# A decoder layer on one core: six small sums of weight magnitudes are put later into TensorE's queue

## The chip, the cores and the metric

The kernel is one program on one core of a Trainium2 chip. Its engines are TensorE (PE, with its weight loads shown apart as PEld), VectorE (DVE), ScalarE (ACT), GpSimd (POOL) and SyncE (SP), which issues most of the DMAs. The metric is the device time of one execution in microseconds (us); less is better.

## What is computed

One decoder layer for 2 sequences of 512 rows, width 512, in three parts, each followed by a residual sum and a layer norm:

```
q, k, v = (x @ (codes * scales) + bias for q, k, v)          # 16 heads of 128, weights in fp4 blocks
attn = softmax(q k^T / sqrt(128));  x = ln(x + (attn v) @ (wo_codes * wo_scales) + bo)
s = coef * (x Wq) ctx^T; keep the 54 largest of 1024; x = ln(x + softmax(s) ctx Wo)
x = ln(x + (silu(x Wg) * (x Wu)) @ Wd)                       # 2048 inner columns
```

The change is in the first part alone, the self-attention.

## The kernel before

**Numbers as sums of two.** To keep float32 accuracy with fast matmuls, each operand is split into a high part in a reduced format and a low part, what is left. A product is then three matmuls: high by high, high by low, low by high. Weights that are a code times a power of two fit into the high part whole, and their low part is zero. The kernel finds this out as it runs: `check_lo` notes each low part of a weight, `run_checks` (L235) has ScalarE sum its absolute values over a row (tile `JA` is thrown away, the sum goes to a column of `mag`), and `run_sums` adds the columns over the 128 partitions with a small float32 matmul (L247, `p<-mag,ones`, two passes, so two records) and lets ScalarE reduce the 2 or 4 results to one number, `flag` (L250, output `fsum`). A projection (`mm_if`, and `bias_o` at L468 for the bias row) loads the flag into a register of TensorE's sequencer (L109, TENSOR_LOAD) and branches over the low matmuls when it is zero (L113, COMPARE_AND_BRANCH). With this data it is zero each time.

**Keys.** A key names a piece of weights: `("qk", j)` for the query and key weights of a head, `("v", g)` for the value weights of four heads, `("o", p)` for the output projection weights of two heads, p = 0 to 7. There are 30 keys, and so 30 sums, 8 of them of kind `o`.

**Order.** The program builds one queue per engine, in the order of one Python loop, and each engine runs its queue strictly in that order; semaphores are waited for at the instruction that needs them. The loop runs over i = 0 to 127. A step j = i // 4 handles one head of one sequence, and qt = i % 4 is its quarter (128 query rows). In quarter i TensorE gets, as far as they exist: `proj_qk` for head step j+1 (qt 0 and 1; tile `R`), `av` for step j-1 (qt 0; `PT,V`), `proj_o` for an earlier pair of steps (qt 2 and 3; `WO,OT`), `proj_v` (`WV,R`), the transposes of quarter i (L528, `ident,PR`), and the scores of quarter i+2 (`QK`). Then come, in this order, the splitting of results by VectorE, `run_sums` when qt is 1, 2 or 3, `bias_o` in three quarters (i = 25, 57, 89, each for two p), the softmax exponentials (L511), and `run_checks`.

**ScalarE and VectorE around it.** For each quarter ScalarE writes the high part of the transposed probabilities (L535, `PT<-p`) and VectorE their low part (L538, `PT<-p,PT`); `av` needs all four quarters of both. VectorE writes the low parts of queries and keys (L373). ScalarE also converts the high parts of coming weights (L277).

**Banks.** `fbank()` hands out four accumulator banks in turn (P[4] to P[7]) to the projections, `av`, the sums and `bias_o`; a user waits for what emptied the bank of the user four before it.

**Where the `o` sums stand.** The checks of `("o", p)` are done in quarter i = 16p+6 for p = 0 to 5, a quarter with qt = 2, and the sum follows in the next quarter, i = 16p+7. The first `proj_o` with these weights is in quarter i = 16p+10, and `bias_o` in i = 16p+9 for odd p.

Of the kernel before, what the change touches and what calls it, by code (L numbers as in the profile page):

```python
# [51 lines left out]
def flat(ws):  # L52
    out = []
    for w in ws:
        if w is None:
            continue
        if isinstance(w, list):
            out += flat(w)
        else:
            out.append(w)  # L60
    return out

def decoder_layer(nc, xT, xn, wq, sq, wk, sk, wv, sv, wo, so, bqk, bv, bo,
                  xwq, xwo, ctxT, ctxn, scal, wg, wu, wd, rq, rk, out):
    with ExitStack() as top:
# [6 lines left out]
        def op(q, fn, *waits):  # L73
            return q.add(fn, flat(waits), True)
# [52 lines left out]
        def sbt(ctx, name, shape, dt=F32):  # L127
            return ctx.enter_context(nc.sbuf_tensor(name, shape, dt))
# [20 lines left out]
        fsum = sbt(top, "fsum", [1, 4])  # L149
        flag = sbt(top, "flag", [1, 32])  # L150
# [70 lines left out]
        now = [-1]  # L221
        checks, sums = [], []
# [16 lines left out]
                    sums.append((now[0], key))  # L239

        def run_sums():
            while sums and sums[0][0] < now[0]:
                _, key = sums.pop(0)
                n, col, ts = FL[key]
                k, ps = fbank()
                o = ps[0:1, 0:n]
                t = pe.add(lambda e, o=o, col=col, n=n: e.matmul(o, ones[:, 0:1], mag[:, col % 4, 0:n],  # L247
                                                                 start=True, stop=True),
                           flat([ts, t_one, bank[5 + k]]), True)
                t = op(act, lambda e, o=o, col=col, n=n: e.activation(fsum[:, 0:n], o, ACT.Copy,  # L250
                                                                       accum_out=flag[:, col:col + 1]),
                       t, T.get(("flag", col - 1)))
                bank[5 + k] = T[("flag", col)] = t

        def flag_of(key):
            c = FL[key][1]
# [65 lines left out]
        T = {}  # L322
        bank = [None] * 8
        nf = [1]

        def fbank():
            k = nf[0] % 4 - 1
            nf[0] += 1
            return k, P[5 + k][:, :]
# [769 lines left out]
        for i in range(4 * NJ):  # L1099
# [25 lines left out]
            if qt:  # L1125
                run_sums()
# [29 lines left out]
            if i == 1:  # L1156
                t = op(act, lambda e: e.activation(bv_r[:, :, 0], bv_f, ACT.Copy), T_BIAS)
# [17 lines left out]
            if j == 30 and qt in (1, 2):  # L1175
                for r in (2 * qt - 2, 2 * qt - 1):
                    k, _ = fbank()
# [4 lines left out]
            if i in (123, 124):  # L1182
                for m in (2 * (i - 123), 2 * (i - 123) + 1):
                    k, _ = fbank()
# [3 lines left out]
            if i in (125, 126):  # L1188
                for hf in range(2):
                    k, _ = fbank()  # L1190
# [256 lines left out]
```

How the kernel before makes its waits and increments, by code:

```python
    def emit(self, eng):  # L38
        reached = {}
        for waits, fn, inc in self.items:
            for sem, v in waits:
                if reached.get(id(sem), 0) < v:
                    reached[id(sem)] = v
                    eng.wait_ge(sem, v)
            if fn is None:
                continue
            ins = fn(eng)
            if inc:
                ins.then_inc(self.sem, 1)
# [33 lines left out]
            def load(self, dst, src, *waits, q=sp):  # L83
                self.n += 1
                s = self.sem
                q.add(lambda e: e.dma_start(dst, src).then_inc(s, 16), flat(waits), False)
                return (s, 16 * self.n)
```

## Time and profile before

| | |
|---|---|
| median of 3 runs | 970.06 us (968.97 to 971.03) |
| profiled execution: its own time | 969.82 us |
| profiled execution: span of its instructions | 968.0 us |
| TensorE busy in the span | 928.3 us (96%) |
| DVE, ACT, POOL busy | 577.2, 580.5, 474.3 us |
| granted TensorE clock, mean | 0.993 of full |
| self-attention with the 30 sums | about 37 to 494 us of the span |

The profile is one execution. Rows of the timeline give the start of an instruction or of a run of like instructions, its length, the engine, the line, and in brackets how long the engine had been idle before it and what it then waited for. Matmuls overlap by design, so distances are read from start to start.

### The profile page before, as it was taken

What the parts mean: (1) busy time and instruction counts of PE and PEld (TensorE: products, weight loads), DVE (VectorE), ACT (ScalarE), POOL (GpSimd) and SP (SyncE); (2) the same over time, 40 slices, a digit from 0 to 9 for tenths busy, and PEclk for the clock granted to TensorE, in tenths of its full rate; (3) what the DMA queues carried; (4) which work ended last, traced back from release to release, by engine and by line L of the source; (5) the groups of instructions that cost most, each with busy time, mean ns of one, the idle gap of its engine ahead of it and who ended that gap; (6) DMA issues with size and microseconds to landing.
All of it is one profiled execution on the core that took longest, in us unless ns stands there. A gap on an engine that the chain in (4) does not pass through costs nothing.

```text
span 968.0 us, 13297 instructions
## 1 busy us (share of the span) xinstructions
PE 928.3 (96%) x4516; PEld 752.3 (78%) x4516; DVE 577.2 (60%) x1057; ACT 580.5 (60%) x1201; POOL 474.3 (49%) x375
## 2 busy tenths in 40 slices
PE   9999899999999999999999989899999899999997
PEld 7787678877788776877667777888878788788886
DVE  5666856576566666565676799984878214511114
ACT  4667866687767778687775446544564634443333
POOL 4246642535515456466564347552684652354440
PEclk9999999999999999999999999989999999999999
DMA  6531220122201322122222122231433241243331
GB/s 197 153 108 46 82 88 1 46 71 71 82 17 28 88 58 68 61 65 60 62 66 87 44 66 88 88 98 55 131 110 96 78 142 43 76 133 97 99 87 43
DMA packets 46101, 76.97 MB, mean 80 GB/s; under 512 B 5584, under 2 KB 11216, under 8 KB 45776
## 3 DMA queue, kind: packets, MB, share of 16 engines
q1 hardware_dynamic: 45600, 75.68, 26.4%
q8 instruction: 41, 0.67, 0.3%
q10 hardware_dynamic: 432, 0.39, 0.1%
q14 instruction: 28, 0.23, 0.1%
HBM read 73.69 MB, written 2.36 MB: 79 GB/s over the span
## 4 chain that ended last, share of the span: by engine, by line
PE 81%; DVE 9%; ACT 5%; issue 3%; DMA 1%; POOL 0%; SPq 0%; DVEq 0%; ACTq 0%; POOLq 0%
PE p L99 75%; PE p L528 5%; DVE JK L503 2%; DVE acc L447 1%; ACT PR L511 1%; ACT JA L235 1%; DVE PT L538 1%; DMA acc<-in_xT 1%; DVE m L726 1%; DVE QK L373 1%; DVE st L588 0%; PE p L779 0%; PE p L636 0%; DVE SX L737 0%; DVE SCL L731 0%
## 5 line engine op out<-in xcount | busy, mean ns | idle before, releaser
L503 DVE TENSOR_SCALAR_CACHE_REDUCE JK<-p,ssc 128x512 bf16<-128x512 f32 x112 | 83.8, 748 | 149.4 <-PE p L99 149.0
L654 POOL TENSOR_TENSOR V<-RAW,V 128x512 fp32r<-128x512 f32 x64 | 82.4, 1309 | 143.2 <-ACT V L653 143.2
L444 POOL TENSOR_TENSOR acc<-SX,acc 128x512 f32<-128x512 f32 x52 | 68.7, 1321 | 169.7 <-ACT SX L438 131.2
L99 PE MATMUL p<-R 128*128 128x512 f32 x544 | 136.9, 394 | 2.4 <-DVE V L399 0.8
L99 PE MATMUL p<-QK 128*128 128x512 f32 x384 | 117.4, 414 | 4.5 <-DVE QK L373 4.1
L99 PEld LDWEIGHTS p<-R 128*128 128x128 f32 x544 | 100.9, 188 | 26.8 <-issue 1.4
L511 ACT ACTIVATE PR<-p,nms,ssc 128x512 f32<-128x512 f32 x112 | 87.2, 778 | 57.6 <-DVE JK L503 57.1
L99 PE MATMUL p<-R,V 128*128 128x512 f32 x480 | 112.7, 390 | 0.8 <-ACT C L653 0.8
L99 PEld LDWEIGHTS p<-R,V 128*128 128x128 f32 x480 | 89.9, 188 | 19.8 <-issue 1.2
L275 POOL TENSOR_TENSOR RAW<-RAW,SCL 128x512 f32<-128x512 f32 x65 | 87.8, 1357 | 28.1 <-DMA SCL<-in_so 14.5
L654 POOL TENSOR_TENSOR C<-RAW,C 128x512 fp32r<-128x512 f32 x58 | 76.0, 1323 | 40.3 <-ACT C L653 40.2
L99 PE MATMUL p<-PT,V 128*128 128x512 f32 x384 | 93.5, 392 | 1.9 <-DVE PT L538 1.9
L99 PE MATMUL p<-C 128*128 128x512 f32 x384 | 92.5, 390 | 0.2 <-issue 0.2
L99 PE MATMUL p<-WV,R 128*128 128x512 f32 x368 | 91.1, 394 | 1.4 <-DVE JK L503 1.1
L99 PE MATMUL p<-V 128*128 128x512 f32 (+1 forms) x432 | 91.3, 368 | 0.7 <-POOL V L654 0.7
L887 DVE TENSOR_TENSOR SX<-p,SX 128x512 f32<-128x512 f32 x32 | 22.1, 691 | 116.5 <-PE p L99 115.7
L538 DVE TENSOR_TENSOR PT<-p,PT 128x512 fp32r<-128x512 f32 x128 | 87.4, 683 | 4.9 <-ACT PT L535 4.7
L99 PEld LDWEIGHTS p<-PT,V 128*128 128x128 f32 x384 | 70.7, 188 | 20.2 <-issue 2.5
L99 PEld LDWEIGHTS p<-V 128*128 128x128 f32 x432 | 74.9, 190 | 14.2 <-ACT V L653 1.1
L99 PEld LDWEIGHTS p<-C 128*128 128x128 f32 x384 | 71.7, 188 | 15.3 <-issue 0.6
L99 PEld LDWEIGHTS p<-WV,R 128*128 128x128 f32 x368 | 67.7, 188 | 19.0 <-issue 3.0
L528 PE MATMUL p<-ident,PR 128*128 128x128 f32 x512 | 77.6, 274 | 0.0
(170 smaller groups left out, 1665.6 us busy)
## 6 DMA issues: line engine op xcount, KB each, us to landing
RAW<-in_wg SPq DMA_DIRECT2D x32, 256.0 KB, 2.8
RAW<-in_wu SPq DMA_DIRECT2D x32, 256.0 KB, 2.6
RAW<-in_ctxn SPq DMA_DIRECT2D x32, 256.0 KB, 2.8
RAW<-in_wd SPq DMA_DIRECT2D x32, 256.0 KB, 2.7
RAW<-in_wq SPq DMA_DIRECT2D x19, 256.0 KB, 2.7
RAW<-in_wk SPq DMA_DIRECT2D x18, 256.0 KB, 2.6
RAW<-in_wv SPq DMA_DIRECT2D x16, 256.0 KB, 2.7
RAW<-in_wo SPq DMA_DIRECT2D x16, 256.0 KB, 4.7
```

What stands on the lines that cost most here:

```text
L99: return e.matmul(outp, a, b, start=st, stop=sp_)
L235: T[("JA",)] = op(act, lambda e, lo=lo, m=m: e.activation(JA[:, :], lo, ACT.Abs, accum_out=m), tl, T.get(("JA",)), T.get(("flag", col - 4)))
L275: tm = op(em, lambda e: e.tensor_tensor(rv, rv, sv_, ALU.mult), td, ts)
L373: tl = op(dve, lambda e: e.scalar_tensor_tensor(out=lo, in0=ps, scalar=bias, in1=hi, op0=ALU.add, op1=ALU.subtract), th, free, T_BQK)
L444: pool, lambda e: e.tensor_tensor(a, buf, a, ALU.add), ts, T[("acc", r)])
L447: bank[5 + k] = T[("scaled", j)] = T[("acc", r)] = op(dve, lambda e: e.scalar_tensor_tensor(out=a, in0=ps, scalar=s, in1=a, op0=ALU.mult, ...
L503: tm = op(dve, lambda e: e.tensor_scalar(JK[:, :], ps, nsc, None, ALU.mult, ALU.min, accum_out=m), T[("S", i)], T.get(("max", i - 1)), T.g ...
L511: T[("exp", i)] = op(act, lambda e: e.activation(PR[:, i % 2, :], ps, ACT.Exp, bias=m, scale=sc, accum_out=rs[:, i % 8:i % 8 + 1]), T[("ma ...
L528: t = pe.add(lambda e, c=c: e.transpose(tp[:, c], PR[:, i % 2, c], ident[:, :]), flat([T[("exp", i)], free, t_id]) if kt == 0 else [], kt ...
L538: tl = op(dve, lambda e: e.tensor_tensor(lo, tv, hi, ALU.subtract), th, fr)
L654: tl = op(pool, lambda e: e.tensor_tensor(lo, raw, hi, ALU.subtract), th, free)
L887: t = op(dve, lambda e: e.tensor_tensor(hf, u, hf, ALU.mult), T[("g", n, 1)], t)
```

## The change

In quarters, the six sums of kind `o` with p = 0 to 5 may be put into the queues only from the second quarter after their last check on, not from the first. Since the quarter with qt = 0 has no `run_sums`, they move from i = 16p+7 to i = 16p+9. All other sums keep their places, and a sum that is ready may now pass one that is held back. The second edit follows from this: ScalarE's small reduction waits for the last one before it in the queue (they share the tile `fsum`) instead of the one with the next lower column. No instruction is added or removed.

```
         def run_sums():
-            while sums and sums[0][0] < now[0]:
-                _, key = sums.pop(0)
+            ready = [e for e in sums if e[0] < now[0] - (e[1][0] == "o" and e[1][1] < 6)]
+            for e in ready:
+                sums.remove(e)
+                key = e[1]
                 n, col, ts = FL[key]
                 k, ps = fbank()
...
-                       t, T.get(("flag", col - 1)))
-                bank[5 + k] = T[("flag", col)] = t
+                       t, T.get(("fsum",)))
+                bank[5 + k] = T[("flag", col)] = T[("fsum",)] = t
```

In the rows of order below, line numbers behind L247 are two higher in the kernel after (the sum is L249 there, its register load still L109, or L470 for L468); `[waits s_act]` means a wait for ScalarE, `s_dve` for VectorE, `s_pool` for GpSimd; `x3` is three like instructions; the matmuls between COMPARE_AND_BRANCH and UNCONDITIONAL_BRANCH are the ones that are skipped.

**The old place, odd p** (TensorE, end of quarter 23 and start of quarter 24, p = 1; p = 3 and 5 alike). `QK` is the last scores of quarter 23, `R` the projection of quarter 24. Before:

```order
L99 MATMUL p<-QK 128x512 x3
L247 MATMUL p<-mag,ones 1x2 [waits s_dve,s_act]
L109 TENSOR_LOAD flag
L99 MATMUL p<-R 128x512 x7
L113 COMPARE_AND_BRANCH
L115 MATMUL p<-R 128x512 x4
```

After:

```order
L99 MATMUL p<-QK 128x512 x3
L109 TENSOR_LOAD flag
L99 MATMUL p<-R 128x512 [waits s_dve]
L99 MATMUL p<-R 128x512 x6
L113 COMPARE_AND_BRANCH
L115 MATMUL p<-R 128x512 x4
```

The sum and its wait for the check are gone from between the scores and the projection.

**The new place, odd p** (TensorE, end of quarter 25, p = 1; p = 3 and 5 alike). The sum `1x4` is that of the value weights, `WO,bv_r` is `bias_o`, whose two register loads take the flags of p = 0 and p = 1. Before:

```order
L99 MATMUL p<-QK 128x512 x3
L247 MATMUL p<-mag,ones 1x4 [waits s_act]
L99 MATMUL p<-WO,bv_r 2x512 [waits s_dve]
L468 TENSOR_LOAD flag
L472 COMPARE_AND_BRANCH
L474 MATMUL p<-WO,bv_r 2x512 x2
L472 UNCONDITIONAL_BRANCH
L99 MATMUL p<-WO,bv_r 2x512
L99 MATMUL p<-WO,bv_r 2x512 [waits s_pool]
L468 TENSOR_LOAD flag
L472 COMPARE_AND_BRANCH
```

After:

```order
L99 MATMUL p<-QK 128x512 x3
L249 MATMUL p<-mag,ones 1x2
L249 MATMUL p<-mag,ones 1x4 [waits s_dve,s_act]
L99 MATMUL p<-WO,bv_r 2x512 [waits s_dve]
L470 TENSOR_LOAD flag
L474 COMPARE_AND_BRANCH
L476 MATMUL p<-WO,bv_r 2x512 x2
L474 UNCONDITIONAL_BRANCH
L99 MATMUL p<-WO,bv_r 2x512
L99 MATMUL p<-WO,bv_r 2x512 [waits s_pool]
L470 TENSOR_LOAD flag [waits s_act]
L474 COMPARE_AND_BRANCH
```

The sum stands in front of the one of the value weights, and the second register load of `bias_o` has a wait for ScalarE.

**The new place, even p** (TensorE, end of quarter 41 and start of quarter 42, p = 2; p = 0 and 4 alike). `WO,OT` is the first `proj_o` with these weights. Before:

```order
L528 MATMUL p<-ident,PR 128x128 x3
L99 MATMUL p<-QK 128x512 x3
L109 TENSOR_LOAD flag
L99 MATMUL p<-WO,OT 128x512 [waits s_pool]
L113 COMPARE_AND_BRANCH
```

After:

```order
L530 MATMUL p<-ident,PR 128x128 x3
L99 MATMUL p<-QK 128x512 x3
L249 MATMUL p<-mag,ones 1x2 [waits s_dve]
L109 TENSOR_LOAD flag [waits s_act]
L99 MATMUL p<-WO,OT 128x512 [waits s_dve,s_pool]
L113 COMPARE_AND_BRANCH
```

The sum stands directly ahead of the load of its own flag, and that load has a wait for ScalarE.

## Rows read from the trace of the kernel before

**Rows 1.** The page: share of the chain that ended last, by engine.

```profile
PE 81%; DVE 9%; ACT 5%; issue 3%; DMA 1%; POOL 0%; SPq 0%; DVEq 0%; ACTq 0%; POOLq 0%
```

**Rows 2.** Waits of TensorE: who for whom, us in total, times, longest.

```profile
PE p L247 <- ACT JA L235: 3.3, 4, 1.0
```

**Rows 3.** Timeline, old place of p = 1: start, length, engine, what, [idle <-releaser].

```profile
117.17 0.85 PE L99 MATMUL p<-QK 128*128 128x512 f32 x3
...
118.49 0.21 ACT L235 ACTIVATION_READ_ACCUMULATOR JA<-WO 128x1 f32 x1
...
118.79 0.19 PE L247 MATMUL p<-mag,ones 128*1 128x2 f32 x2 [0.77 <-ACT JA L235]
...
119.17 2.09 PE L99 MATMUL p<-R 128*128 128x512 f32 x8 [0.19 <-issue]
...
119.62 0.60 ACT L535 ACTIVATE PT<-p 128x512 fp32r<-128x512 f32 x1
...
120.26 0.68 DVE L538 TENSOR_TENSOR PT<-p,PT 128x512 fp32r<-128x512 f32 x1
...
121.06 2.61 PEld L99 LDWEIGHTS p<-PT,V 128*128 128x128 f32 x12 [0.23 <-DVE PT L538]
```

**Rows 4.** Timeline, the same order of work without a sum in between.

```profile
200.81 0.85 PE L99 MATMUL p<-QK 128*128 128x512 f32 x3
...
201.50 1.99 PE L99 MATMUL p<-R 128*128 128x512 f32 x8
...
203.33 2.89 PE L99 MATMUL p<-PT,V 128*128 128x512 f32 x12
```

**Rows 5.** Timeline, old place of p = 2.

```profile
186.95 0.84 PE L99 MATMUL p<-QK 128*128 128x512 f32 x3
...
189.80 2.89 PE L99 MATMUL p<-PT,V 128*128 128x512 f32 x12
```

**Rows 6.** Timeline, after the old place of p = 0.

```profile
62.71 0.69 DVE L538 TENSOR_TENSOR PT<-p,PT 128x512 fp32r<-128x512 f32 x1 [1.22 <-ACT PT L535]
...
63.51 2.69 PEld L99 LDWEIGHTS p<-PT,V 128*128 128x128 f32 x12
```

**Rows 7.** Timeline, the kernel's first sum, directly ahead of its own flag's load.

```profile
36.89 0.16 ACT L250 ACTIVATE fsum<-p 1x4 f32<-1x4 f32 x1
...
37.96 0.70 PE L99 MATMUL p<-WV,R 128*128 128x512 f32 x2 [1.10 <-DVE JK L503]
```

**Rows 8.** The register loads of line 109: count, shortest, median, longest in ns.

```profile
L109 PEldq TENSOR_LOAD <-flag x51: 296/303/503, 37.2 to 548.7; - x51
```

**Rows 9.** Timeline, new place of p = 2.

```profile
195.50 0.60 PE L528 MATMUL p<-ident,PR 128*128 128x128 f32 x4
...
195.85 0.95 PE L99 MATMUL p<-QK 128*128 128x512 f32 x3
...
196.62 0.59 ACT L535 ACTIVATE PT<-p 128x512 fp32r<-128x512 f32 x1
196.63 1.08 PE L99 MATMUL p<-WO,OT 128*128 128x512 f32 x4
...
197.56 0.60 PE L528 MATMUL p<-ident,PR 128*128 128x128 f32 x4
...
198.41 0.93 PE L99 MATMUL p<-QK 128*128 128x512 f32 x3 [0.25 <-DVE QK L373]
```

**Rows 10.** Timeline, new place of p = 1, and the quarter behind it.

```profile
128.85 0.59 ACT L535 ACTIVATE PT<-p 128x512 fp32r<-128x512 f32 x1
...
129.14 0.08 PEld L99 LDWEIGHTS p<-WO,bv_r 128*2 128x2 f32 x1 [0.56 <-issue]
...
129.38 0.18 ACT L250 ACTIVATION_READ_ACCUMULATOR fsum<-p 1x1 f32 x1
...
129.52 1.24 PE L99 MATMUL p<-WO,OT 128*128 128x512 f32 x4
...
132.69 0.60 ACT L396 ACTIVATE V<-p 128x512 fp32r<-128x512 f32 x1 [1.19 <-PE p L99]
```

## The prediction

> **What bounds the kernel now.** I read the page first: in the chain that ended last TensorE has 81% [rows 1], so time is lost or won where TensorE is held up, and a microsecond on another engine counts only if TensorE then waits. Next the waits of TensorE: the small sums (L247) cost it 3.3 us in 4 waits for ScalarE's checks [rows 2]. Three of these four are the old places of p = 1, 3 and 5 (118.79, 243.18 and 367.62 us of the span, the same picture each time); the fourth, at 466 us, is not moved. So 2.3 us is what the change can aim at. The third view is the timeline at each old and each new place, on TensorE, ScalarE and VectorE together, to see what is late next. The old places of p = 0, 2 and 4 have no wait at all.
>
> **Part 1, the old places of odd p (3 of them).** TensorE starts the scores at 117.17, idles 0.77 us until ScalarE's second check has ended at 118.49 + 0.21 = 118.70, does the sum, and starts the projection at 119.17 [rows 3]. Without a sum in between, the projection starts 201.50 - 200.81 = 0.69 us behind the scores [rows 4], here at 117.86. So the projection will start 1.31 us earlier. But the next work is `av`, and its weight load at 121.06 already stands idle for 0.23 us until VectorE has written the low part of quarter 23's probabilities, at 120.26 + 0.68 = 120.94. That in turn follows ScalarE's high part at 119.62, which stands in ScalarE's queue behind the check and two conversions; ScalarE has no idle time from the check to there [rows 3], and nothing in it waits for TensorE. Taking the sum away does not shorten that queue, for ScalarE's reduction of this sum comes behind the high part. Without the sum `av` would be ready 2.52 us behind the scores (203.33 - 200.81 [rows 4]), at 119.69, and must then wait until 121.06. The wait only changes its name, from the check to VectorE's `PT`. Gain: 0. The other end is 1.31 us each, if that row were no real gate; I take 0, since the gate is in the row itself.
>
> **Part 2, the old places of even p (3 of them).** No wait here, only the work of the sum. From scores to `av` it is 189.80 - 186.95 = 2.85 us with the sum [rows 5] and 2.52 without [rows 4]: 0.33 us for p = 2, and the same for p = 4. For p = 0 the `av` load at 63.51 comes 0.11 us behind the end of VectorE's low part (62.71 + 0.69 = 63.40) [rows 6], the distance that a load held up by it has at 121.06 (0.12), so it is at its gate too, and the gain is 0. Together -0.66 us. Bounds: 0 and 3 x 0.33 = 1.0.
>
 For p = 2: scores from 195.85 to 196.80, then the sum (0.19 us, [rows 3]), done at about 197.0. ScalarE is in the middle of its high part, begun at 196.62 [rows 9]. Where a reduction follows such a part, its result is read out 129.38 + 0.18 - 128.85 = 0.71 us after the part began [rows 10], here at 197.33. The register load takes 0.30 us in the median [rows 8], which gives 197.63 as the earliest start of `proj_o`. The latest comes from the only place of the kernel before where a sum stands directly ahead of its flag: there 1.07 us pass from the start of the reduction to the matmul (37.96 - 36.89 [rows 7]), of which at least 0.18 is the reduction, so at most 0.89 lies behind the flag: 198.22. That row has other waits in it, and its load was the slowest of 51 at 0.50 us, if the longest is the first; I take 197.75, near the lower end. Before, `proj_o` started at 196.63, so it is 1.12 us late. Its four matmuls take 1.24 us behind a fresh load [rows 10] against 1.08 [rows 9]: 0.16 more. Part of this is given back: the scores at 198.41 had to wait for VectorE's `QK` anyway. Transposes and scores are 195.85 - 195.50 = 0.35 apart when nothing waits, so these scores could have started at 197.56 + 0.35 = 197.91 and have 0.50 us of slack [rows 9]. What stays is 1.12 + 0.16 - 0.50 = 0.78 us, the work of the sum included. VectorE's maximum, the exponential and everything behind them hang on these scores. I take p = 0 and 4 at the same: 3 x 0.78 = 2.34. Bounds for one: 1.00 - 0.50 = 0.50 and 1.59 + 0.16 - 0.50 = 1.25.
>
> The Trainium skill ("Runtime: NRT & Kernel Launch", Instruction fetch mechanics) puts a register load by TENSOR_LOAD at about 200 ns. The median here is 303 ns [rows 8], so the trace does not agree, and the row is used. By the page the two new places would be 0.1 us cheaper each, 0.6 us in all.
>
> **Part 4, the new places of odd p.** Here `bias_o` follows, and its second register load takes the flag of just this sum. ScalarE reaches the reduction behind its high part of 128.85, as it does now for the sum of the value weights, and the new one stands first: flag at 129.38 + 0.18 = 129.56 [rows 10]. From there the register load and the branch have to pass. Now they leave 0.56 us idle before the last weight load of `bias_o`, at 129.14 [rows 10], when nothing waits; so that load comes at 129.56 + 0.56 = 130.12 at the earliest, and by the 0.89 us of above at 130.45. That is 0.98 to 1.31 us late. I take 1.05, near the lower end, for there is only one wait. `proj_o` at 129.52 keeps its distance and is 1.05 us late as well. The second sum (0.33 us) and the bank of this `proj_o`, which is now the one that VectorE empties after the key projection, are hidden behind that wait. Does anything absorb it? ScalarE idles 1.19 us for TensorE in the next quarter, at 132.69 [rows 10], so it has nothing queued that could hold TensorE up independently; the delay goes on to the end. 3 x 1.05 = 3.15. Bounds: 2.9 and 3.9.
>
> **Part 5, the rest.** The `fsum` wait: two reductions stand back to back on ScalarE in quarters 25, 57 and 89, where the exponential comes a few tenths later; TensorE's loss is larger, and covers it. DMAs, GpSimd and their queues keep their order. Cost 0.
>
> **The sum.** 0 - 0.66 + 2.34 + 3.15 = 4.83 us. The profiled execution, 969.82 us by its own time, would be 974.65; the median of the runs is 0.24 above it, so the forecast is 970.06 + 4.83 = 974.9 us. Its own range, with all bounds of parts 2 to 4 and the extremes not all on one side, is 973.6 to 976.6.
>
> **The rivals.**
> (a) *The removed waits count after all, beside the new ones.* It takes that the `av` gate of part 1 moves ahead with TensorE. Then -3 x 1.31 = -3.93 comes on top: 970.06 + 4.83 - 3.93 = 971.0, and 970.9 to 972 by bounds. Against it: ScalarE's unbroken queue in rows 3.
> (b) *The odd new places are absorbed.* If a later gate that does not hang on TensorE swallows the 1.05 us, as the `QK` wait does 0.50 of in part 3, what is left is 2.34 - 0.66 = 1.7: 971.7. Against it: the 1.19 us for which ScalarE waits for TensorE.
 Then the old odd places win 1.31 and the new ones cost 0.33: -3 x 0.98 = -2.9, the even places even out: 967.1. It decides by whether the queue ahead of the load lasts as long as the way of the flag. Against it: behind the first sum TensorE stood idle for 1.10 us [rows 7], and in the new places the scores ahead of the sum have begun to end when the sum starts. The Trainium skill speaks for this side: "Perfetto Trace Analysis" (Identifying Performance Opportunities, Optimization Strategy) says to find the gaps of the busiest engine and to let what ends them come sooner, and rows 3 has such a gap.
> (d) *Dearer.* Both late starts at their upper bounds everywhere, and an exponential that comes late shifts ScalarE's order against TensorE once more: 3 x 1.25 + 3.9 - 0 = 7.7, 977.7.
>
> **How the numbers follow.** The forecast has 0.74, (a) 0.07, (b) 0.08, (c) 0.06, (d) 0.05. Predicted is the forecast's 974.9. The range goes from the lower end of (a), 970.9, to the upper end of the forecast's own, 976.6, and leaves out (c), (d) and a little of the forecast's. About 0.2%, 1.9 us, is what a measurement of this kernel can tell from no change: faster by more is (c), 0.06; within it are (a) and (b), 0.15; slower is the forecast and (d), 0.79.
>
> **What the profile after would show.** Part 1: no sum at the old place, the projection 0.69 us behind the scores, and `av` idle for over 1 us for VectorE's `PT`, at the same distance from the scores as before (3.9 us). Parts 3 and 4: idle time of about 0.9 us on TensorE between the moved sum and `proj_o` in three places, and about 1.5 us before the last weight load of `bias_o` in three. The waits of TensorE for the check (L235) fall to one of 1.0 us. From quarter 25 on every row is later by the sum so far, and the granted clock is the same. I am wrong if `av` moves ahead with the projection (a), if the distance from `proj_o` in quarter 26 to the next steps shrinks (b), or if the loads of the flags leave no idle time (c).

## The result, and the profile after

| | before | after |
|---|---|---|
| median (lowest to highest), us | 969.21 (966.88 to 971.03), 6 runs | 974.53 (973.07 to 975.04), 6 runs |
| profiled execution: own time, span, mean clock | 969.82, 968.0, 0.993 | 975.04, 973.2, 0.992 |

The kernel after takes 1.0049 times as long, with a 95% interval of 1.0033 to 1.0064: 5.3 us more between the medians, 5.2 between the two spans. The forecast was 974.9 us. All runs here and below are of the same, undisturbed state.

The page of the kernel after, its span, the busy times, and the chain that ended last ([rows 1] of before):

```profile
span 973.2 us, 13290 instructions
...
PE 928.7 (95%) x4516; PEld 752.7 (77%) x4516; DVE 578.1 (59%) x1057; ACT 581.9 (60%) x1201; POOL 474.1 (49%) x375
...
PE 77%; DVE 11%; ACT 6%; issue 3%; DMA 1%; POOL 1%; SPq 0%; DVEq 0%; ACTq 0%; POOLq 0%
```

TensorE is busy for 928.7 us against 928.3: the work is the same, and the loss is idle time. TensorE's share of the chain fell from 81% to 77%, and VectorE and ScalarE took it over. Line numbers of the helpers are two higher than before (the sum is L249, its reduction `fsum` L252).

Waits of TensorE, whole execution: who for whom, us in total, times, longest.

```profile
PE p L99 <- DVE PT L540: 6.2, 8, 1.3
...
PE p L99 <- DVE JK L505: 3.7, 4, 1.1
PE p L99 <- ACT fsum L252: 3.1, 3, 1.0
```

The wait of [rows 2], the sum for the check, is down from four times to the one at 466 us that was not moved. In its place stand three waits of 1.0 us for the sum's own reduction, `fsum`, and three of the four for `JK` (the fourth stands behind the kernel's first sum, [rows 7]). The waits for `PT`, 1.9 us in four before, are 6.2 us in eight: the three old places of odd p and the one of p = 0.

**The old place of p = 1** (timeline; [rows 3] of before):

```profile
118.14 0.85 PE L99 MATMUL p<-QK 128*128 128x512 f32 x3
...
118.83 1.99 PE L99 MATMUL p<-R 128*128 128x512 f32 x8
...
120.57 0.73 DVE L505 TENSOR_SCALAR_CACHE_REDUCE JK<-p,ssc 128x512 bf16<-128x512 f32 x1
120.59 0.59 ACT L537 ACTIVATE PT<-p 128x512 fp32r<-128x512 f32 x1
...
121.23 0.68 DVE L540 TENSOR_TENSOR PT<-p,PT 128x512 fp32r<-128x512 f32 x1
...
122.06 3.01 PE L99 MATMUL p<-PT,V 128*128 128x512 f32 x12 [1.25 <-DVE PT L540]
```

The projection now starts 0.69 us behind the scores, as forecast. But `av` starts 3.92 us behind them (122.06 - 118.14), and before it was 3.93 us (121.10 - 117.17), by this row of the kernel before ([rows 3] has the weight load of it at 121.06):

```profile
121.10 3.01 PE L99 MATMUL p<-PT,V 128*128 128x512 f32 x12
```

The wait has changed its name and has kept its end. It is the same at p = 3 and p = 5.

**The new place of p = 2** (timeline; [rows 9] of before):

```profile
197.50 0.95 PE L99 MATMUL p<-QK 128*128 128x512 f32 x3
...
198.38 0.19 PE L249 MATMUL p<-mag,ones 128*1 128x2 f32 x2
...
198.80 0.18 ACT L252 ACTIVATION_READ_ACCUMULATOR fsum<-p 1x1 f32 x1
...
199.47 0.84 PEld L99 LDWEIGHTS p<-WO,OT 128*128 128x128 f32 x4 [1.00 <-issue]
199.50 1.25 PE L99 MATMUL p<-WO,OT 128*128 128x512 f32 x4 [0.93 <-DVE JK L505]
```

The reduction ends at 198.98, and the first weight load of `proj_o` comes 0.49 us behind it, with the register load in between. The profile names `DVE JK` as the releaser, but `JK` is no input of `proj_o`. This matmul does wait for VectorE too, for its bank; in e4_oldflag below, with the same bank and no wait for the flag, it starts 1.00 us behind the scores with no idle time, against 1.99 us here. So the line of weight loads, which says "issue", has the truer label: the sequencer was busy with the flag. The next scores start 3.44 us behind these (200.94, no wait any more); before it was 2.56 [rows 9]. The place costs 0.88 us. For p = 0 and 4 the idle times are 0.81 and 0.90 us.

**The new place of p = 1** (timeline; [rows 10] of before):

```profile
129.10 0.24 PE L249 MATMUL p<-mag,ones 128*1 128x2 f32 x4
129.27 0.86 PE L99 MATMUL p<-WO,bv_r 128*2 128x512 f32 x3
...
130.33 0.18 ACT L252 ACTIVATION_READ_ACCUMULATOR fsum<-p 1x1 f32 x1
...
131.16 0.08 PEld L99 LDWEIGHTS p<-WO,bv_r 128*2 128x2 f32 x1 [1.58 <-issue]
131.16 0.40 PE L99 MATMUL p<-WO,bv_r 128*2 128x512 f32 x1 [1.03 <-ACT fsum L252]
...
131.54 1.25 PE L99 MATMUL p<-WO,OT 128*128 128x512 f32 x4
...
132.62 1.55 PE L99 MATMUL p<-WV,R 128*128 128x512 f32 x6
```

The flag is there at 130.51, and the last matmul of `bias_o` starts 0.65 us later. From the first sum to the next projection (`WV,R`) pass 3.52 us; before it was 130.59 - 128.14 = 2.45, by these rows of the kernel before:

```profile
127.27 0.95 PE L99 MATMUL p<-QK 128*128 128x512 f32 x3
127.37 0.19 ACT L235 ACTIVATION_READ_ACCUMULATOR JA<-WV 128x1 f32 x1
...
128.14 0.19 PE L247 MATMUL p<-mag,ones 128*1 128x4 f32 x2
...
130.59 2.07 PE L99 MATMUL p<-WV,R 128*128 128x512 f32 x8
```

The place costs 1.07 us, and 1.08 and 1.12 for p = 3 and 5.

### The profile page after: what moved, and what is told of

It is laid out like the page before. It is cut to its first block, busy times and chain, and to the rows that moved or that the text cites. A ratio compares the mean times of both kernels' runs of the same rounds, so it can differ in the third digit from the quotient of the medians.

```text
span 973.2 us, 13290 instructions
## 1 busy us (share of the span) xinstructions
PE 928.7 (95%) x4516; PEld 752.7 (77%) x4516; DVE 578.1 (59%) x1057; ACT 581.9 (60%) x1201; POOL 474.1 (49%) x375
## 4 chain that ended last, share of the span: by engine, by line
PE 77%; DVE 11%; ACT 6%; issue 3%; DMA 1%; POOL 1%; SPq 0%; DVEq 0%; ACTq 0%; POOLq 0%
PE p L99 71%; PE p L530 4%; DVE JK L505 2%; DVE acc L449 1%; DVE PT L540 1%; ACT JA L235 1%; ACT PR L513 1%; DMA acc<-in_xT 1%; DVE m L728 1%; DVE WV L283 1%; ACT PT L537 1%; DVE st L590 1%; DVE QK L375 1%; POOL C L656 1%; ACT QK L372 0%
## 5 line engine op out<-in xcount | busy, mean ns | idle before, releaser
L277 POOL TENSOR_TENSOR RAW<-RAW,SCL 128x512 f32<-128x512 f32 x65 | 87.4, 1351 | 28.5 <-DMA SCL<-in_so 14.1
L99 PE MATMUL p<-WO,OT 128*128 128x512 f32 x256 | 75.4, 416 | 5.7 <-DVE acc L449 2.8
```

The source lines that it names most:

```text
L99: return e.matmul(outp, a, b, start=st, stop=sp_)
L277: tm = op(em, lambda e: e.tensor_tensor(rv, rv, sv_, ALU.mult), td, ts)
```

## The experiments

The forecast's theory: the price is the way of the flag (matmul, ScalarE's reduction, register load, branch), for which TensorE stands still at the new place; the waits removed at the old place were no gain, since `av` was held up by others. Against it stand the rivals (a) and (c), that the removed waits count, and (b), that a part of the delay is absorbed. The loss of each place is read as a local distance in the timeline, since the first 30 us alone differ by up to 1.9 us from one execution to another. Ratios are to runs of the kernel before on the same chip in the same batch.

**One half each.** Hold back the sums of even p alone (e1_even), of odd p alone (e2_odd).

```
-            ready = [... (e[1][0] == "o" and e[1][1] < 6)]
+            ready = [... (e[1][0] == "o" and e[1][1] in (0, 2, 4))]     # e1_even
+            ready = [... (e[1][0] == "o" and e[1][1] in (1, 3, 5))]     # e2_odd
```

> Only the sums of p = 0, 2 and 4 are late, in the quarter 16p+9, directly ahead of the load of their own flag; p = 1, 3 and 5 stand as before. Theory (each place has its own price): -0.66 us at the old places, +2.34 at the new ones, so 1.7 us slower than the kernel before (0.17%); the profile of the changed kernel gives 0.87 - 0.36 for p = 2 and 0.82 - 0.35 for p = 4, and 1.1 for p = 0, of which 0.36 came from a late DMA, so 1.7 to 2.1. Rival (the whole loss belongs to bias_o): 0, within 0.3 us of before. Rival (only the work of the sum moves, the even places are neutral and all gain of the odd ones is missing here): 0.

> Only the sums of p = 1, 3 and 5 are late, in quarter 16p+9, ahead of bias_o. Theory: nothing won at the old places, since av is held by VectorE's PT, and 1.05 to 1.1 us lost at each new one: 3.2 us slower than before (0.33%), with TensorE idle for 1.0 us for ScalarE's fsum ahead of the last matmul of bias_o three times. Rival (a, the removed waits count): 3.2 - 3.9 = 0.7 us faster than before. Rival (bias_o is absorbed): 0.

e1_even: 970.61 us (969.48 to 973.98), ratio 1.0017 (1.0006 to 1.0028), so +1.6 us. TensorE has the same four waits for `JK` as the kernel after (3.7 us), none for `fsum`, and the old waits for the check:

```profile
PE p L249 <- ACT JA L235: 3.3, 4, 1.0
```

e2_odd: 972.07 us (970.34 to 974.02), ratio 1.0028 (1.0016 to 1.0040), so +2.7. Its timeline at the new place of p = 1:

```profile
129.33 0.39 PE L99 MATMUL p<-WO,bv_r 128*2 128x512 f32 x1 [1.03 <-ACT fsum L252]
```

The halves carry their own waits, and both cost: the places add up, 1.6 + 2.7 = 4.3 us against 4.7 for the whole by its ratio, well within the intervals. In e2_odd `av` keeps its distance (gain 0 three times), and the new places cost 1.06 to 1.12 us each. Rivals (a) and (b) have no room left: (a) would have made e2_odd 0.7 us faster than the kernel before, (b) as fast.

**The way of the flag.** As after, but `proj_o` and `bias_o` take a flag that has long been there. The sums stay where they are and are still reduced. What this kernel leaves out is that these branches follow their own weights; with this data the flag is zero either way.

```
-            f, t_f = flag_of(("o", p))
+            f, t_f = flag_of(("v", 0))          # in proj_o and in bias_o
```

> The changed kernel, but all output projections and bias_o branch by the flag of the first value weights, which is ready since the start, and not by their own (its value is the same with this data, so the same matmuls run; what is left out is that these branches follow their own weights). All sums and reductions stay in the queues at their late places, only nobody waits for the six. Theory (the price is the way of the flag): the idle 0.9 us ahead of proj_o and the 1.0 us in bias_o go, each late sum costs 0.33 us of work, at the even places inside the 0.50 us slack of the scores: 3 x 0.33 - 0.66 = +0.3 us against before, 4.5 to 5 us under the changed kernel. Rival (the price is the shifted banks and ScalarE's two reductions in a row): as the changed kernel, +4.8 us against before.

969.42 us (967.10 to 970.52), ratio 0.9996 (0.9986 to 1.0005). The same place as above, in e4_oldflag:

```profile
127.23 0.24 PE L249 MATMUL p<-mag,ones 128*1 128x2 f32 x4
...
128.96 1.24 PE L99 MATMUL p<-WO,OT 128*128 128x512 f32 x4 [0.41 <-DVE QK L375]
```

The idle 1.03 us are gone, and so is the whole loss of 0.49%. A new sum at these places, without the wait for its flag, costs 0.35 us at odd p (the bank of this `proj_o` then waits for VectorE's `QK`, which the forecast had hidden behind the flag) and nothing at even p, where it lies in the slack of the scores (the next scores start 2.55 us behind these at p = 2 and 4, as before). The way of the flag is the price of the change: the places of the sums, the banks and ScalarE's reductions are the same in this kernel as in the kernel after.

**Can the old wait be won at all?** The sums of odd p in quarters 24, 56 and 88, which normally have no `run_sums`: behind the check's wait, and a quarter ahead of `bias_o`.

```
-            if qt:
+            if qt or i in (24, 56, 88):
                 run_sums()                      # with the line of e2_odd
```

> The sums of p = 1, 3 and 5 are one quarter late only (quarters 24, 56 and 88, which have no sums otherwise), behind av and the scores: the wait for the check is gone and the flag is ready long before bias_o; the even ones stand as before. This takes the old wait away without the new one. Theory: av starts at the same distance from the scores as before, so nothing is won there, and the sum costs its 0.33 us of work at a place without slack: +1.0 us against the kernel before (0.10%), idle time for PT ahead of av about 1.2 us. Rival (a, the removed waits count, 1.31 us each): -3.9 + 1.0 = 2.9 us faster than before (0.30%).

969.87 us (967.72 to 971.83), ratio 1.0004 (0.9993 to 1.0015). Timeline of e3_odd24 (its scores start at 115.56):

```profile
117.98 0.73 DVE L505 TENSOR_SCALAR_CACHE_REDUCE JK<-p,ssc 128x512 bf16<-128x512 f32 x1
118.02 0.59 ACT L537 ACTIVATE PT<-p 128x512 fp32r<-128x512 f32 x1
...
119.48 2.98 PE L99 MATMUL p<-PT,V 128*128 128x512 f32 x12 [1.26 <-DVE PT L540]
```

The rival, a gain of 2.9 us, is out: no sum is late here, nothing waits for a flag, and still `av` starts 3.92 us behind the scores. The cost was 0.4 us instead of 1.0, because the sum's 0.30 us in quarter 24 are partly given back at `bias_o`; why is shown further down.

**Who holds `av`?** The forecast had named ScalarE's queue. So its check of quarter 22 goes to quarter 23 (e5_check23). In the rows above, though, VectorE's low part also follows directly behind its own `JK`, and that one behind a low part of `WV`; so this low part goes a quarter later (e7_low23), and both together (e6_both).

```
         def run_checks():
+            if now[0] in (22, 54, 86):
+                return                          # e5_check23, e6_both
...
-            flush()
+            if i not in (22, 54, 86):
+                flush()                         # e7_low23, e6_both
```

e5_check23 and e6_both keep the sums as in the kernel before, e7_low23 builds on e3_odd24; all three have the sum in quarters 24, 56, 88.

> As the kernel with the odd sums in quarters 24, 56 and 88, and in addition ScalarE's second check of these weights comes a quarter later (23, 55, 87), behind quarter 23's high part of the probabilities. This asks what holds av: before, ScalarE's high part ended at 120.22 and VectorE's maximum of the scores, which stands ahead of the low part in its queue, at 120.33. Theory 1 (both engines are late, VectorE last): ScalarE's high part comes 0.6 us earlier, VectorE's low part does not, av starts as before, so the time is that of the kernel with the odd sums in 24, +0.04% against before. Theory 2 (ScalarE alone paces it, as the prediction's part 1 told it): av 0.6 us earlier three times, 1.9 us faster than that kernel, -0.15% against before.

> As the kernel with the odd sums in quarters 24, 56 and 88, and in addition VectorE's (and GpSimd's) low parts of the weights converted in quarters 22, 54 and 86 come a quarter later, so that VectorE reaches the low part of the probabilities about 0.8 us earlier, while ScalarE's check stays where it is. Both theories: ScalarE's high part still ends at 120.2, so av does not move; +0.04% against before. If VectorE alone were the gate: 0.6 to 0.8 us earlier three times, about -0.2% against before.

> Both of the other two at once: the check and VectorE's low part of the value weights each a quarter later, the odd sums in quarters 24, 56 and 88. Theory 1 (two engines late together): only now av starts earlier, by 0.6 us at each of three places, 1.9 us under the kernel with the odd sums in 24, so -0.15% against before (range -0.25 to -0.05%, as the moved work may come late elsewhere). If it is as slow as each alone, something else holds av.

Timeline of e5_check23, then of e7_low23 (its scores start at 117.26), then of e6_both, at this place:

```profile
116.12 0.85 PE L99 MATMUL p<-QK 128*128 128x512 f32 x3
...
117.95 0.61 ACT L537 ACTIVATE PT<-p 128x512 fp32r<-128x512 f32 x1
...
118.54 0.74 DVE L505 TENSOR_SCALAR_CACHE_REDUCE JK<-p,ssc 128x512 bf16<-128x512 f32 x1
...
119.20 0.68 DVE L540 TENSOR_TENSOR PT<-p,PT 128x512 fp32r<-128x512 f32 x1
...
120.03 2.99 PE L99 MATMUL p<-PT,V 128*128 128x512 f32 x12 [1.25 <-DVE PT L540]
```

```profile
118.78 0.74 DVE L505 TENSOR_SCALAR_CACHE_REDUCE JK<-p,ssc 128x512 bf16<-128x512 f32 x1
...
119.71 0.59 ACT L537 ACTIVATE PT<-p 128x512 fp32r<-128x512 f32 x1
...
121.17 3.01 PE L99 MATMUL p<-PT,V 128*128 128x512 f32 x12 [1.24 <-DVE PT L540]
```

```profile
116.52 0.85 PE L99 MATMUL p<-QK 128*128 128x512 f32 x3
...
118.04 0.74 DVE L505 TENSOR_SCALAR_CACHE_REDUCE JK<-p,ssc 128x512 bf16<-128x512 f32 x1
118.36 0.60 ACT L537 ACTIVATE PT<-p 128x512 fp32r<-128x512 f32 x1
...
118.99 0.69 DVE L540 TENSOR_TENSOR PT<-p,PT 128x512 fp32r<-128x512 f32 x1 [0.21 <-ACT PT L537]
119.83 3.01 PE L99 MATMUL p<-PT,V 128*128 128x512 f32 x12 [0.65 <-DVE PT L540]
```

| behind the start of the scores, us | ScalarE's high part ends | VectorE's `JK` ends | `av` starts |
|---|---|---|---|
| before, after, e3_odd24 | 3.05 | 3.16 | 3.92 or 3.93 |
| e5_check23 | 2.44 | 3.16 | 3.91 |
| e7_low23 | 3.04 | 2.26 | 3.92 |
| e6_both | 2.44 | 2.27 | 3.31 |

Two engines hold `av`, and they reach the low part within 0.11 us of each other. Freeing either one alone moves it by 0.02 us at most, freeing both by 0.61.

Yet the times are 969.79 us (967.50 to 970.84), ratio 0.9995 (0.9983 to 1.0008) for e5_check23, 972.01 (970.41 to 974.13), 1.0024 (1.0012 to 1.0036) for e7_low23, and 969.85 (968.03 to 972.94), 1.0005 (0.9993 to 1.0018) for e6_both. For e7_low23 and e6_both these are misses: 1.0004 and 0.9985 were expected, so each lost some 2 us somewhere else.

**Where the gain of e6_both went.** Timeline of e6_both, quarter 25:

```profile
126.33 0.95 PE L99 MATMUL p<-QK 128*128 128x512 f32 x3
...
126.86 0.19 ACT L237 ACTIVATION_READ_ACCUMULATOR JA<-WV 128x1 f32 x1
...
127.21 0.19 PE L249 MATMUL p<-mag,ones 128*1 128x4 f32 x2
...
128.93 1.27 PE L99 MATMUL p<-WO,OT 128*128 128x512 f32 x4
```

and the register loads of `bias_o` in the same stretch, by their line (count: shortest, median, longest ns, first and last start), in e6_both and in e3_odd24:

```profile
L470 PEldq TENSOR_LOAD <-flag x2: 298/299/300, 127.2 to 127.9; - x2
```

```profile
L470 PEldq TENSOR_LOAD <-flag x2: 295/296/297, 126.0 to 126.8; - x2
```

The sum of the value weights stands ahead of `bias_o` and waits for their last check, and the sequencer gets to the register loads only behind it. In e6_both this check ends at 127.05, 0.72 us behind the start of the scores, and the first load begins at 127.2, when the scores are about to end (126.33 + 0.95 = 127.28); in e3_odd24 it ends 0.03 us ahead of the scores (125.92 to 125.95), and both loads pass while matmuls that came before them keep the array busy, with no idle time on TensorE. The late low part made the check late. The kernel before lies between the two: its check ends 0.29 us behind the scores (127.56 to 127.27). The distance from this sum to `proj_o` follows it:

| us, in quarters 25, 57, 89 | check ends behind the scores | sum to `proj_o` | sum to next projection |
|---|---|---|---|
| e3_odd24 | -0.03 | 1.06, 1.05, 1.08 | 2.34, 2.38, 2.33 |
| before | 0.29 | 1.38, 1.33, 1.37 | 2.45, 2.45, 2.56 |
| e6_both | 0.72 | 1.72, 1.74, 1.77 | 2.83, 2.85, 2.96 |
| e7_low23 | 0.72 | 1.72, 1.73, 1.83 | 2.83, 2.83, 3.04 |

That closes both sums. In e6_both a place brings 0.61 at `av`, the sum in quarter 24 costs 0.30, and the last column 0.4: nothing is left. In e7_low23 the 0.61 is missing, and 3 x 0.7 = 2.1 us or 0.21% remain; measured 0.24%.

**One more gate, and the check put ahead.** e8_o7 is e6_both with the sum of the last key (p = 7), and the `bias_o` behind it (that of p = 6 and 7, in quarter 112 before), a quarter later at the end of the attention. e9_early is e8_o7 with one of the checks of quarters 24, 56 and 88 put in front of the exponential, and e10_early_alone is the kernel before with that edit alone.

```
-        def run_checks():
-            for _ in range(2):
+        def run_checks(most=2):                               # e9_early, e10_early_alone
+            for _ in range(most):
...
-            if qt or i in (24, 56, 88):
+            if qt and i != 111 or i in (24, 56, 88, 112):     # e8_o7, e9_early
                 run_sums()
-            if j % 8 == 6 and qt == 1 and j < 24 or i == 112:
+            if j % 8 == 6 and qt == 1 and j < 24 or i == 113: # e8_o7, e9_early
...
                 scores(i + 2)
+            if i in (24, 56, 88):
+                run_checks(1)                                 # e9_early, e10_early_alone
             evacs()
```

> The kernel with check and low parts late, and in addition the fourth wait of 0.97 us at a sum, that of p = 7 in quarter 111, is taken away in the same manner: its sum goes to quarter 112, and the bias_o that takes its flag from 112 to 113. The av behind it starts at 468.29 now and could start at 467.71 by VectorE's PT (467.59), so by the theory of gates 0.58 us are won and 0.33 us of work come back in quarter 112: 0.25 us under the kernel without this edit (0.03%, which the times cannot tell, the profile can). By the rival that the whole wait counts, 1.3 - 0.33 = 1.0 us.

> e8_o7 with one of the checks of quarters 24, 56 and 88 put ahead, behind ScalarE's high part and in front of the small reduction. Reading behind it: from the sum of the value weights in quarters 25, 57 and 89 to proj_o pass 1.38 us in the kernel before, 1.06 in e3_odd24 and e5_check23, and 1.72 in e6_both, e7_low23 and e8_o7; and the last check that this sum needs ends 0.29 us behind the start of the scores in the kernel before, 0.03 ahead of it in e3_odd24, 0.72 behind it in e6_both. The first register load of bias_o begins about 0.1 to 0.2 us behind that end. Theory: this check sets the distance, for the sequencer gets to the loads only behind it. Then the check now ends about 0.1 us ahead of the scores, the distance falls to about 1.06 us, and with 3 x 0.66 = 2.0 us less the ratio to the kernel before is about 0.9965. Rival: GpSimd's low part or the two register loads themselves hold it, the distance stays at 1.72, and the ratio is that of e8_o7, 0.9986.

> The kernel before with nothing changed but one of the checks of quarters 24, 56 and 88 put ahead of the exponential, into 0.85 us in which ScalarE stands idle. Theory: the check that the sum of the value weights waits for ends over 1 us sooner, the distance from this sum to proj_o falls from 1.38 to 1.06 us in three places, and the time by 0.95 us, ratio 0.9990. The scores-to-av distance of quarters 23 and 24 stays 3.92 us. Rival: the distance is not set by the check and stays at 1.38, ratio 1.0000. The timing can hardly tell these two apart, the trace can.

e8_o7: 968.14 us (967.07 to 971.07), ratio 0.9986 (0.9976 to 0.9997). At quarter 112 `av` starts 3.54 us behind the scores instead of 4.10, as expected; it waits 0.76 us for VectorE's `PT` there.

e9_early: 967.35 us (966.36 to 967.98), ratio 0.9985 (0.9976 to 0.9994). Its timeline in quarter 25:

```profile
126.41 0.19 ACT L237 ACTIVATION_READ_ACCUMULATOR JA<-WV 128x1 f32 x1
126.64 0.95 PE L99 MATMUL p<-QK 128*128 128x512 f32 x3
...
127.52 0.19 PE L249 MATMUL p<-mag,ones 128*1 128x4 f32 x2
127.64 1.10 PE L99 MATMUL p<-WO,bv_r 128*2 128x512 f32 x4
128.57 1.39 PE L99 MATMUL p<-WO,OT 128*128 128x512 f32 x4
```

The check ends at 126.60, 0.04 us ahead of the scores, and the distance from the sum to `proj_o` is 1.05 us in all three places. e10_early_alone: 968.33 us (966.21 to 971.42), ratio 0.9997 (0.9986 to 1.0009), and the distance is 1.05 us too, from 1.38; its check ends 1.45 us ahead of the scores, and being so early brings nothing more. The check is what sets it, as long as it is late; the rivals (GpSimd's low part, the loads as such) are out. But a distance to `proj_o` is not a time. Its four matmuls, when their branch is no longer hidden, take 0.1 to 0.2 us longer to the next projection, and from the sum to that one pass 2.34 us in both kernels, against 2.88, 2.85 and 2.99 in e8_o7 and 2.45, 2.45 and 2.56 before: 0.5 to 0.65 and 0.1 to 0.2 us a place stay. The expectations, 0.9965 and 0.9990, had counted the whole. With what stays, 1.7 us in all, e9_early should be 0.18% below e8_o7. The two ran in different batches, at 0.9985 and 0.9986, and their intervals do not settle it.

**What the traces say of the whole part.** The traces do settle it. The distance from the scores issued in quarter 8 (behind the old place of p = 0) to the last ones, issued in quarter 125, takes in every other place and leaves out the start and the later parts of the layer. It is 463.32 us in the kernel before; the others differ from it by:

| kernel | in the trace, us | by the ratio of the times, us |
|---|---|---|
| after | +5.02 | +4.7 (3.2 to 6.2) |
| e1_even | +1.80 | +1.6 (0.6 to 2.7) |
| e2_odd | +3.09 | +2.7 (1.5 to 3.9) |
| e4_oldflag | +0.23 | -0.4 (-1.4 to 0.5) |
| e3_odd24 | +0.53 | +0.4 (-0.7 to 1.5) |
| e5_check23 | +0.56 | -0.5 (-1.6 to 0.8) |
| e7_low23 | +2.24 | +2.3 (1.2 to 3.5) |
| e6_both | +0.47 | +0.5 (-0.7 to 1.7) |
| e8_o7 | -0.12 | -1.4 (-2.3 to -0.3) |
| e9_early | -1.80 | -1.5 (-2.3 to -0.6) |
| e10_early_alone | -0.41 | -0.3 (-1.4 to 0.9) |

The halves add up to 4.89 of the 5.02 us, and e9_early is 1.68 us below e8_o7, where 1.7 was worked out from the local distances. The gain of e9_early over the kernel before, of 0.15 to 0.19%, is shown by times and trace alike. That of e8_o7 is shown by its times alone: the trace has 0.1 us, just outside their interval, and what the rest is stays open. By the ratios both beat the kernel after by 0.6%.

## Why the forecast was right, point by point

**Part 1, the old places of odd p: 0.** Measured 0 three times, and rival (a) had 1.31 each. The reason given was half of the truth: ScalarE's queue does hold `av`, but VectorE's holds it too, 0.11 us later. With e5_check23 alone one would have called that reason wrong, with e6_both it is seen to be one of two.

**Part 2, the old places of even p: -0.66.** p = 2 gave -0.36 and p = 4 between -0.35 and -0.39 (forecast -0.33 each), read from the lag of TensorE's instructions behind those of the kernel before. At p = 0 the projection gained 0.2, and `av` stands 0.35 us further behind the scores (4.12 us against 3.77) instead of level: in this execution a multiplication on GpSimd (L277, L275 before), which waits for a DMA, and with it ScalarE's conversion started 0.35 us later (60.59 against 60.24 us), ahead of any moved instruction. It is not put down to the change. Over all twelve traces this multiplication starts between 0.19 and 0.81 us behind the scores, and where the sum is gone `av` follows it: 4.12 us in the kernel after, 3.95 in e1_even, 3.51 in e4_oldflag. The forecast's reading that `av` of the kernel before stood at VectorE's gate there was wrong: with the sum in place it starts at 3.77 us also where VectorE is later (e2_odd, low part done at 3.62 instead of 3.48) or earlier (e9_early, 3.38). The gain of that place is between 0.26 us and nothing, as the DMA lands.

**Part 3, the new places of even p: +0.78 each.** Measured 0.87, 0.88 and 0.82, by the lag behind the kernel before. For p = 2 `proj_o` is 199.50 - 198.28 = 1.22 us late (its place would be 0.78 us behind the scores, [rows 9]), against 1.12 forecast; the fresh branch and the slack of 0.50 us are as read. The range given was 0.50 to 1.25.

**Part 4, the new places of odd p: +1.05 each.** Measured 1.07, 1.08 and 1.12. That nothing absorbs it was right as well: the lag stays on to the end. The cover that the forecast gave to the sum and its bank is real, and e4_oldflag shows its price without it, 0.35 us.

**The sum.** 0 - 0.73 + 2.57 + 3.27 = 5.1 us, against 4.83 forecast and 5.3 between the medians. That the forecast of the time, 974.9, came within 0.4 us of the 974.53 measured is in part luck: it started from the median of three runs, 970.06, which is 0.85 us above that of six, and its sum was 0.5 us short. Each part lies within its own bounds. **Rival (c)**, the sequencer running ahead and the flag's way hidden, failed on the idle time of 0.81 to 1.05 us in all six places. The Trainium skill ("Perfetto Trace Analysis", Identifying Performance Opportunities, Optimization Strategy) has one find the gaps of the busiest engine; the trace does show the gap of [rows 3], and e3_odd24 that closing it alone brings nothing, since two other engines end at the same point.

## What to carry to other kernels

A wait is worth only its distance to the next one: before a stall is removed, look in the same rows for what comes up behind it on every engine, and expect more than one, within a tenth of a microsecond. A value that an engine's sequencer must read (a flag for a branch) has to be finished well before the array runs dry, so look at what stands between the producer, its last input and the load. Judge an edit of a few tenths by the distance between the same two instructions across the place, as far as the next work that is the same in both, and not as far as the first that moves.

## What the runs showed of the hardware that was not expected

A fresh result costs TensorE about 1 us when it decides a branch: 0.24 us for the reduction on ScalarE (198.74 to 198.98), 0.30 us for the register load, the rest for the ways between them. When the queue of the sequencer is behind, the four matmuls after a branch take 1.24 to 1.44 us instead of 1.08, so a delay moved from before a branch to behind it is not all won. And two executions of the same instructions are not alike outside the part that was changed. TensorE's first products (128x128) change their pitch from 0.43 to 0.22 us, at 3.8 us in one trace and at 7.0 in another, with the others between; the profile gives the granted clock there as 1.00 before and behind. By 30 us the twelve traces lie up to 1.9 us apart, over a third of what this change cost; the pitch is not the whole of it, for e10_early_alone changes it at 6.6 us and is yet among the earliest at 30. Behind the last scores the program is the same in all twelve, and takes 436.2 to 439.4 us. There the granted clock falls for a few us to its lower level (1.2 GHz), as from 631 to 638 us of the kernel before (0.51, TensorE busy for 5.85 of the 7 us); its mean over this stretch is 0.99 in the three shortest and 0.98 in the three longest. That it makes the difference is not shown. The spans of two profiles set against each other would not have shown effects of 0.1%; distances within one did.
